# Experts' down matrix normed by maxima on VectorE, scale tables on GpSimd, and the norm sums placed inside a TensorE step

## The reference, cut to what matters

```
x: (32, 128, 128)        cond: (32, 8)      shared gate/up: (128, 512), down: (512, 128)
experts: 8, gate/up (128, 512), down (512, 128)

mlp(x, g, u, d) = (gelu(x @ g) * (x @ u)) @ d
w, sel = top_k(softmax(cond), 2);  w = w / sum(w)           # two experts per batch row
out = x + mlp(x, shared) + sum_k w[b, k] * mlp(x[b], expert sel[b, k])
```

## Time and profile before

| | us |
|---|---|
| three runs | 213.44, 214.37, 215.72 (median 214.37) |
| profiled execution, its own time | 213.45 |
| its span | 211.6 |
| granted TensorE clock over the span | 1.00 |
| TensorE busy | 202.7 |
| ScalarE busy | 137.6 |
| VectorE busy | 127.8 |
| GpSimd busy | 107.9 |

### The profile page before, as it was taken

One profiled execution on the slowest core, in us unless ns is written; L12 is line 12 of the kernel. 1 busy time (PEld: TensorE's weight loads), 2 busy tenths in 40 slices (PEclk: granted clock), 3 DMA queues, 4 the chain that ended last, 5 costly groups with the idle time before them and its releaser, 6 DMA issues.

```text
span 211.6 us, 6607 instructions
## 1 busy us (share of the span) xinstructions
PE 202.7 (96%) x2663; PEld 162.8 (77%) x2663; DVE 127.8 (60%) x231; ACT 137.6 (65%) x225; POOL 107.9 (51%) x110
## 2 busy tenths in 40 slices
PE   7999597999989999999999999999999999999995
PEld 2345353544434468899999999999999999999995
DVE  4796986788889999754434434435435344444451
ACT  6356377799997999656556566565565665655650
POOL 3002324446544666765655656556556556565562
PEclk9999999999999999999999999999999999999999
DMA  6999600000000000000010010010010010010011
GB/s 203 402 427 437 268 3 0 2 3 0 0 0 0 0 3 5 0 5 3 3 50 3 3 52 4 0 53 3 5 51 5 0 53 3 5 50 3 3 53 53
DMA packets 2814, 11.70 MB, mean 55 GB/s; under 512 B 353, under 2 KB 609, under 8 KB 2401
## 3 DMA queue, kind: packets, MB, share of 16 engines
q1 hardware_dynamic: 2640, 11.01, 13.0%
q10 hardware_dynamic: 144, 0.26, 0.5%
HBM read 9.18 MB, written 2.10 MB: 53 GB/s over the span
## 4 chain that ended last, share of the span: by engine, by line
PE 68%; ACT 11%; DVE 3%; issue 1%; DVEq 0%
PE o_ps L670 7%; PE u_ps L650 7%; PE g_ps L650 7%; PE o_ps L668 7%; PE u_ps L652 7%; PE g_ps L652 7%; PE o_ps L669 7%; PE u_ps L651 7%; PE g_ps L651 7%; ACT gel L298 3%; ACT wsk L320 3%; ACT h L303 3%; ACT wsk L315 1%; PE o_ps L631 1%; PE o_ps L632 1%; PE o_ps L633 1%
## 5 line engine op out<-in xcount | busy, mean ns | idle before, releaser
L271 POOL TENSOR_TENSOR h<-h 128x512 f16<-128x512 f32 x92 | 106.1, 1159 | 99.2 <-ACT h L303 68.8
L453 DVE SCALAR_TENSOR_TENSOR h<-gel,sk_factor,u_ps 128x512 f32<-128x512 f32 x64 | 47.8, 747 | 66.5 <-PE u_ps L652 35.3
L298 ACT ACTIVATE gel<-g_ps,sk_gate 128x512 f32<-128x512 f32 x64 | 44.0, 687 | 48.8 <-PE g_ps L652 48.8
L303 ACT CAST h<-h 128x512 f16<-128x512 f32 x92 | 56.4, 613 | 4.9 <-DVE h L453 4.6
L652 PE MATMUL g_ps<-x,wsk 128*128 128x128 f16 x256 | 46.2, 219 | 0.0
L652 PE MATMUL u_ps<-x,wsk 128*128 128x128 f16 x256 | 46.2, 219 | 0.0
L651 PE MATMUL g_ps<-x,wsk 128*128 128x128 f16 x256 | 46.2, 219 | 0.0
L651 PE MATMUL u_ps<-x,wsk 128*128 128x128 f16 x256 | 46.2, 219 | 0.0
L650 PE MATMUL g_ps<-x,wsk 128*128 128x128 f16 x256 | 46.1, 219 | 0.0
L650 PE MATMUL u_ps<-x,wsk 128*128 128x128 f16 x256 | 46.1, 219 | 0.0
L670 PE MATMUL o_ps<-h,wsk 128*128 128x128 f16 x256 | 45.9, 219 | 0.0
(11 more groups left out here) (107 smaller groups left out, 307.2 us busy)
## 6 DMA issues: line engine op xcount, KB each, us to landing
wsk<-skills SPq DMA_DIRECT2D x3, 2048.0 KB, 16.5
outT<-xT SPq DMA_DIRECT2D x7, 256.0 KB, 2.0
xT<-xT SPq DMA_DIRECT2D x2, 768.0 KB, 6.8
wsh<-shared SPq DMA_DIRECT2D x3, 256.0 KB, 3.8
xT<-xT ACTq DMA_DIRECT2D x1, 256.0 KB, 3.4
xT<-xT SPq DMA_DIRECT2D x1, 256.0 KB, 5.2
outT<-xT SPq DMA_DIRECT2D x1, 192.0 KB, 2.8
outT<-xT SPq DMA_DIRECT2D x1, 64.0 KB, 1.6
```

The costliest lines, as they stand in the source:

```text
L271: nc.gpsimd.tensor_tensor(hidden_lo(t), hidden_full(t), hidden_hi(t), ALU.subtract).then_inc(lo_ok, 1)
L298: nc.scalar.activation(gel[:, t % NG, :], g_ps[t % 2][:, :], ACT.Gelu_apprx_tanh, scale=scale).then_inc(gelu_ok, 1)
L303: nc.scalar.copy(hidden_hi(t), hidden_full(t)).then_inc(hi_ok, 1)
L453: nc.vector.scalar_tensor_tensor(out=h32[:, t % N32, :], in0=gel[:, t % NG, :], scalar=factor, in1=u_ps[t % 2][:, :], op0=ALU.mult, op1=AL ...
```

## The change

The down norm of the experts is found by four absolute maxima per partition on VectorE in place of four squares on ScalarE. The tables move to GpSimd. Group 0 of x is computed first. VectorE's steps for maxima, masks and routing are rearranged; TensorE sums the norms between a step's gate and up halves (after the down product) and no longer after the up half.

```diff
-        FIRST, X_NEXT, X_REST, K_GATE, K_UP, K_DOWN = range(6)
-        XA = 4
+        XF, XA = 2, 5
+        FIRST, X_NEXT, K_GATE, X_REST, K_UP, K_DOWN = range(6)
-            return (t // C + G - 1) % G
+            return t // C
-        TOP_AT = {1: (1,), 3: (2, 3), 5: (4, 5), 6: (6, 7)}
-        K_STEPS = [5, 9]
-        MASK_AT = {3: X_NEXT, 6: X_REST, 8: K_GATE, 12: K_UP, 22: K_DOWN}
-        SPREAD_AT = {4: X_NEXT, 7: X_REST, 9: K_GATE, 13: K_UP, 23: K_DOWN}
-        SQUARES_AT = {11: 0, 13: 1, 17: 2, 21: 3}
+        TOP_AT = {1: (2,), 3: (3, 4), 10: (5,), 11: (6, 7)}
+        PART_AT = {14: 0, 16: 1, 18: 2, 20: 3}
+        K_STEPS = [5, 10]
+        MASK_AT = {3: X_NEXT, 9: K_GATE, 12: X_REST, 14: K_UP, 21: K_DOWN}
+        SPREAD_AT = {4: X_NEXT, 10: K_GATE, 13: X_REST, 15: K_UP, 22: K_DOWN}
+        ROUTED_AT = 11
+        TABLE_AT = {4: X_NEXT, 14: X_REST}
+        SKILL_TABLES_AT = 24
-        X_AT = {5: 1, 8: 7, 9: 2, 10: 3, 15: 4, 19: 5, 23: 6}
+        X_AT = {3: 0, 5: 2, 8: 3, 11: 4, 15: 5, 19: 6, 23: 7}
 # SP queue: no longer the logits; they follow x's first group on ScalarE's queue
-            sp.dma_start(logits[:, :], cond).then_inc(cond_in, 16)
-            act.dma_start(xT32[:, (G - 1) * GN:], xT[:, (G - 1) * GN:]).then_inc(x_in[0], 16)
+            act.dma_start(xT32[:, 0:GN], xT[:, 0:GN]).then_inc(x_in[0], 16)
+            act.dma_start(logits[:, :], cond).then_inc(cond_in, 16)
 # GpSimd: three calls of shared_tables (4 or 5 small operations each), one of skill_tables (6)
+            shared_tables(FIRST)
             for t in range(C, STEPS):
...
                 nc.gpsimd.tensor_tensor(hidden_lo(t), ...).then_inc(lo_ok, 1)
+                if t in TABLE_AT:
+                    shared_tables(TABLE_AT[t])
+                if t == SKILL_TABLES_AT:
+                    skill_tables()
 # VectorE
+            def part_top(n):
+                if n == 0:
+                    dve.wait_ge(sk_in[DOWN], 16)
+                nc.vector.tensor_reduce(parts[:, n:n + 1], wsk32[:, (2 * E + 2 * n) * I:(2 * E + 2 * n + 2) * I], AX.X, ALU.max,
+                                        apply_absolute_value=True).then_inc(part_ok, 1)
             def mask(n):
+                if n == K_DOWN:
+                    dve.wait_ge(part_ok, E // 2)
+                    tops(KC + DOWN, parts[:, :])
...
             probabilities()
-            routing_weights()
             for q in (GATE, UP, DOWN):
                 top_shared(q)
             top_x(0)
+            top_x(1)
             mask(FIRST)
             for t in range(STEPS):
                 hidden(t)      # then x_low, skill_low of step t-1
+                if t in PART_AT:
+                    part_top(PART_AT[t])
                 # then tops of x; scales now ahead of mask
+                if t == C - 1:
+                    routing_weights()
+                    routing_spread()
+                if t == ROUTED_AT:
+                    routed_tables()
-                if t == 10:
+                if t == 7:
                     add_group(0)
 # TensorE
                     half_shared(t, GATE)
                     if down_of(t) >= C and down_of(t) != down_of(t - 1):
                         down_shared(down_of(t))
+                    if t in SPREAD_AT:
+                        spread_norms(SPREAD_AT[t])
                     half_shared(t, UP)
-                if t in SPREAD_AT:
-                    spread_norms(SPREAD_AT[t])
                 if t == ROUTE_AT:
                     pe.wait_ge(r_spread, 2 * TOP_K)
+                    pe.wait_ge(s_step, X_NEXT + 1)
```

More of the change, by code:

```diff
@@ L305, in x_high @@
             def x_high(j):
-                act.wait_ge(scaled, (FIRST if j == 0 else X_NEXT if j < XA else X_REST) + 1)
+                act.wait_ge(scaled, (FIRST if j < XF else X_NEXT if j < XA else X_REST) + 1)
                 nc.scalar.activation(x_part(j, 0), x_full(j), ACT.Copy, scale=sc[:, XC + j:XC + j + 1]).then_inc(x_hi_ok, 1)
[L309 to L315, removed]
             def skill_high(n):
                 kind, w, hi, _ = piece_of(n)
-                act.wait_ge(scaled, K_GATE + kind + 1)
+                act.wait_ge(scaled, K_OF[kind] + 1)
                 nc.scalar.activation(hi, w, ACT.Copy, scale=sc[:, KC + kind:KC + kind + 1]).then_inc(sk_hi_ok, 1)
@@ L334, in _ @@
                     shared_high(GATE)
-                    x_high(0)
+                    x_high(1)
                     shared_high(UP)
@@ L378, in scales @@
                 norm = n_ps[1][:, 0:b - a]
-                if n >= K_GATE:
+                if n in GRAMS:
                     norm = n_all[:, a:b]
-                    nc.vector.tensor_reduce(norm, n_ps[1][:, 0:E // 2 if n == K_DOWN else P], AX.X, ALU.max).then_inc(n_red, 1)
-                    dve.wait_ge(n_red, n - K_GATE + 1)
+                    nc.vector.tensor_reduce(norm, n_ps[1][:, 0:P], AX.X, ALU.max).then_inc(n_red, 1)
+                    dve.wait_ge(n_red, K_OF.index(n) + 1)
                 nc.vector.tensor_scalar(e_bits[:, a:b], norm.bitcast(U32), 1, EXP_MASK,
@@ L534, in _ @@
                         top_x(j)
-                if t in MASK_AT:
-                    mask(MASK_AT[t])
                 if t == 2:
                     shared_low(GATE, 1)
-                    x_low(0)
+                    x_low(1)
                     shared_low(UP, 2)
@@ L543, in _ @@
                 if t in SPREAD_AT:
-                    n = SPREAD_AT[t]
-                    scales(n)
-                    if n == X_NEXT:
-                        shared_tables(1, XA, 2)
-                    if n == X_REST:
-                        shared_tables(XA, G, 3)
-                        inverse_table()
-                if t == C:
+                    scales(SPREAD_AT[t])
+                if t in MASK_AT:
+                    mask(MASK_AT[t])
+                if t == C - 1:
+                    routing_weights()
                     routing_spread()
-                if t == ROUTE_AT + 1:
+                if t == ROUTED_AT:
                     routed_tables()
-                if t == 24:
-                    skill_tables()
-                if t == 10:
+                if t == 7:
                     add_group(0)
@@ L586, in spread_norms @@
                 pe.wait_ge(diag_ok, n + 1)
-                if n < K_GATE:
+                if n not in GRAMS:
                     sums = n_ps[1][:, 0:b - a]
@@ L590, in spread_norms @@
                     nc.tensor.matmul(sums, ones[:, :], top2[:, a:b], start=False, stop=True).then_inc(norm_ok, 1)
-                elif n < K_DOWN:
+                else:
                     nc.tensor.matmul(n_ps[1][:, 0:P], ones[:, :], diag[:, :], start=True, stop=True).then_inc(norm_ok, 1)
-                else:
-                    nc.tensor.matmul(n_ps[1][:, 0:E // 2], ones[:, :], sq_floor[:, :], start=True, stop=True).then_inc(norm_ok, 1)
             def gate_up_first(c, q):
@@ L709, in _ @@
                             pe.wait_ge(sk_in[kind], 16)
-                        if n == 0 and kind == UP:
-                            pe.wait_ge(diag_ok, K_GATE + 1)
+                        if n == 0 and kind:
+                            pe.wait_ge(diag_ok, K_OF[kind - 1] + 1)
                         a = (kind * E + 2 * n) * I
                         for half in range(2):
-                            last = gram(n_ps[0][:, 0:P], wsk32[:, a + half * I:a + (half + 1) * I], n == 0 and half == 0)
+                            last = gram(n_ps[0][:, 0:P], wsk32[:, a + half * I:a + (half + 1) * I],
+                                        n == 0 and half == 0)
                         if n == 3:
```

107 lines of the change are left out of this document (56 added, 51 removed).

## The result

The changed kernel is slower: median 220.63 us of four runs (220.02 to 221.47), the kernel before 213.91. The ratio is 1.0295, 95% interval 1.023 to 1.0359. The forecast was 217.0 with a range of 213.0 to 219.5; slower was right, the size was not, and the time is outside the range. The profiled execution of the changed kernel took 221.47 us, span 219.6, against 213.45 and 211.6. Its mean TensorE clock was 0.984; the three others had 0.991 or 0.992 and took 220.02 to 220.68, so the trace shows a little more loss than the median.

A forecast was written before the change was run, and what follows sets the result against it. TensorE, busy 96% of the span, was taken as the bound, losing time where VectorE is late. Terms 0.4 - 2.8 - 1.15 + 3.3 + 3.6 - 0.35 gave +3.0 us: 216.4 to 217.4, named 217.0, range 213.0 to 219.5.

The forecast's parts named there:

- start, to T(4): Until step 4 begins: logits land late behind x, delaying VectorE's maxima and TensorE's first sum; +0.4 us.
- steps 4 to 8: Early steps: postponed maxima leave VectorE little work, so TensorE runs free; -2.8 us.
- steps 8 to 12: Still ahead, less a 0.65 us stall for the mid-step sum in step 10; -1.15 us.
- steps 12 to 16: VectorE's fuller steps make TensorE stall for two masks; +3.3 us, assuming a shorter routed_tables.
- steps 16 to 24: VectorE's 16.0 us backlog makes TensorE stand at step 22, plus 0.75 for x_low meeting GpSimd; +3.6 us.
- steps 24 to 32: TensorE free, as tables no longer delay VectorE: 14.9 us instead of 15.26, -0.35 us.
- the wait at step 22: TensorE stands 3.65 us at the experts' down sum between the step's halves, waiting for VectorE's mask.
- X_REST wait: Step 13, mid-step: TensorE stalls for VectorE's mask of x's rest; 1.65 us, or 2.55 if routed_tables costs 1.7.
- K_UP wait: Step 15, mid-step: TensorE stalls 1.15 us for VectorE's K_UP mask, behind hidden and part_top.
- Rival 3: GpSimd's small table operations cost as much as a low part: about +2.6 us more, 219.6 us; chance 0.10.
- rival 2: VectorE keeps up, only up-half-to-mask paths count at mid-step sums: -2.3 with early logits, 212.1 us; chance 0.12.
- rival 1: VectorE's backlog and the start are smaller (early logits, cheaper x_low and part_top): +0.6, 215.0 us; chance 0.27.

The follow-up runs named there:

- e2_fill_wait: Changed kernel with 14 matmuls of zeros ahead of the experts' down norm sum in step 22, inside TensorE's wait: 218.4 us, ratio 1.0192.
- f1_before_filled: Kernel before with 16 matmuls of zeros inside TensorE's 2.0 us wait at step 7: 213.63 us against 215.53, ratio 0.9938.
- b1_logits_behind_x: Kernel before with only the logits moved behind x's first group on ScalarE's queue: ratio 1.0023; 215.05 us against 213.07 at full clock.
- c2_best_act: Changed kernel's early order, but squares on ScalarE, sums at step ends, later down mask; logits first on ScalarE's queue, x behind: 210.73 us, ratio 0.9835.
- e3_down_late: Changed kernel with the experts' down mask one step later (22), its sum three later (25), their tables two later (26): 216.82 us, ratio 1.0116.
- c4_down_at_24: Changed kernel's early order, squares on ScalarE, logits first on SP's queue; down mask at 23, sum ending step 24, tables at 25: 212.06 us, ratio 0.9883.
- e1_logits_first: Changed kernel with the logits issued first on SP's queue again, x's first group alone on ScalarE's: 218.27 us, ratio 1.0174.

## Why the prediction was wrong

Its sum, term by term, against the two traces (T of the changed kernel from above, T of before from the earlier trace rows):

| stretch | predicted | measured |
|---|---|---|
| start, to T(4) | +0.4 | +1.40 (17.26 - 15.86) |
| steps 4 to 8 | -2.8 | -2.69 (7.83 - 10.52) |
| steps 8 to 12 | -1.15 | -0.57 (10.43 - 11.00) |
| steps 12 to 16 | +3.3 | +4.12 (11.75 - 7.63) |
| steps 16 to 24 | +3.6 | +5.71 (21.87 - 16.16) |
| steps 24 to 32 | -0.35 | -0.13 (15.13 - 15.26) |
| sum | +3.0 | +7.84 |

**The step that failed is the price of the wait at step 22.** The sum has the wait, but no term for the clock behind it: it was put at nothing without a reason, and it was 2.5 us. Three more terms were too small, by 1.0 (start), 0.8 (steps 12 to 16) and 0.6 (steps 8 to 12); at the start only the size was wrong, and the other two lacked one small wait for GpSimd each.

*Steps 16 to 24.* The wait at step 22 is where it was put, 3.92 us where 3.65 and the 0.75 for x_low, 4.4 together, were expected; VectorE runs without a pause from hidden(15) at 47.53 to the mask at 63.77, 16.2 us against 16.0 and 0.75. One of the two x_low met a low part (1.27 us at 59.42), the other did not (0.76 at 50.81). What the term lacked is the clock: from the up half of step 22 to the start of step 24 TensorE ran at 1.2 GHz. e2_fill_wait prices that at 2.5 us by T(24) and 2.74 by T(32), or 2.2 by the medians. With the wait filled, T(16) to T(24) is 19.37 us (66.63 - 47.26) where 19.75 was predicted, so the rest of the term was right. The prediction named a wait of 3 to 4 us and priced it as if TensorE were as fast behind it as ahead. The row that could have warned was not there: the profiled execution of before had a wait of 2.0 us and a clock of 1.00 throughout. But the runs shown, 213.44, 214.37 and 215.72, were spread wider than the page explained, and the 0.92 between profile and median was taken over without asking what it was. The clocks of these three are not known. Among the 17 executions of the kernel before beside f1_before_filled, 215.72 would lie with those at 0.992 and 213.44 with those at 1.000, and 214.37 between the two.

*The start.* The mechanism was right (the logits late, all maxima behind them, the FIRST sum waits 1.65). They were put at 4.2 and the first maximum at 5.8; they came at 5.34 and 6.87. The 4.1 us for x was its landing time of before, when nothing came behind it; both transfers now took 4.2 us from their issues at 0.72 and 1.15. A part of the miss is luck: T(4) of before, 15.86, is the earliest of four traces with that start, and between the medians of the two starts (16.13 and 17.35) the delay is 1.2 and not 1.4. The Trainium skill, DMA: Bandwidth & Descriptors, Queues, rings and completion order, says that the increment lands after every earlier write of its DMA engine. b1_logits_behind_x, where the logits come at 5.21, agrees, and so does c2_best_act, where they go first on the same queue and are there at 3.2. The rule gives the order, not the size.

*Steps 12 to 16.* The X_REST wait was 1.42 (1.65 predicted); the K_UP wait 1.83 instead of 1.15. The reason, read from the trace, is one small operation: the last of the scales of X_REST began at 43.25 inside a GpSimd low part and took 1.14 us instead of 0.16, so hidden(14) was late by about 0.9. It is the same (1.14 or 1.15 us) in all eleven traces with this order of the steps, and no run takes it away, so its price is not shown by an experiment. The prediction used the lock for x_low, said that the 1.16 us cast of the earlier trace rows began with a GpSimd operation, and gave the scales nothing for it. The Trainium skill, SBUF — State Buffer, Who interferes with whom, names tensor_scalar among the operations that can take part, and says that tensor_reduce on trn2 never does. The trace agrees with both: part maxima beside low parts kept their length (1.20 to 1.21 us).

*Steps 8 to 12.* The K_GATE stall came as predicted (0.48 for 0.65). The down product of step 8 waited 0.41 for GpSimd, which no step of the prediction had.

**What held.** The pause of steps 4 to 8 was worth 2.7 us. part_top costs 1.13 us from start to start (45.09 to 46.22), 1.17 predicted. VectorE takes ScalarE's place as the full engine. GpSimd's small operations mostly took 0.2 to 0.4 us, 3.0 us for the experts' six with one of 1.40; hidden(29) waited 1.8 us for what stood behind them, and TensorE none of it. Rival 3 is out, and so are rival 2 and rival 1.

**The rivals' chances.** 0.59 on slower was right in sign. The upper end of the range, 219.5, came from the GpSimd rival; it should have come from the clock. With a clock drop of 2.5 us in the sum the forecast would have been 219 to 220.

What stays open: why the clock falls behind the same wait in some executions of one kernel and not in others. No run varies it.

## What to carry to other kernels

Price a long idle time of TensorE twice: the wait itself, and the slower matmuls behind it (here 2.5 us behind a wait of 3.9). If a kernel's runs lie in two groups, compare their mean clocks before anything else, and if a wait cannot be removed, fill it with matmuls of zeros: one such loop of 16 took 0.6% off the kernel before.

A sum or a mask that must cross two engines needs a due date behind the backlog of the engine that makes it, at a place where the waiting engine has just finished its own long work (e3_down_late: 1.5 us beyond the clock). In mid-step, the up half behind it feeds the very engine that is late. A later date does not help an engine that is full: c4_down_at_24 won nothing by it.

A transfer of 1 KB that starts the longest chain of small operations goes first on its queue.

## What the runs showed of the hardware

- TensorE's clock was 0.50 from inside a wait of 3.9 us to the start of step 24 (63 to 69.5 us). In the kernel before, the mean clock of an execution is either 1.000 or 0.992, 213.07 and 215.62 us in one set of 23 runs (5 and 18). With its 2.0 us wait filled, it is 1.000 or 0.999 in 12 of 12. The clock does not fall each time in e1_logits_first either, whose profiled execution has a wait of 3.9 us: one of its four runs had 1.000 and took 217.52 us, 1.2 less than the slowest two on average.
- A VectorE operation on 3 columns took 1.14 us, where it otherwise takes 0.16, when begun during a GpSimd low part; a maximum over 1024 columns begun the same way kept its 1.21.
- 1 KB behind 256 KB on ScalarE's queue was there 4.2 us after its issue, first on that queue 2.4 us (c2_best_act), first on SP's queue 1.6 us (the kernel before).
